# Graph attention on one core: key weights and x alternate in the load queue, a second bank and stage for the last two folded quads, and a reordered opening and tail

## The reference

```python
h = relu(layernorm(x))                     # no scale, no shift, eps 1e-5
q, k, v = h @ W_q.T + b_q, h @ W_k.T + b_k, h @ W_v.T + b_v
z = (q @ k.T) / sqrt(512) * adj
z = where(z == 0, -10000, z)
out = x + relu(softmax(z, axis=1) @ v)
```

## Time and profile before

| | us |
|---|---|
| runs, median of 3 | 1481.22 (1480.55 to 1481.66) |
| the profiled execution's own time | 1482.13 |
| its span in the profile | 1480.3 |
| PE busy | 1461.4 (99%) |
| DVE busy | 1301.0 (88%) |
| ACT busy | 868.7 (59%) |
| POOL busy | 44.7 (3%) |
| moved by DMA | 301.24 MB, mean 203 GB/s |

### The profile page before, as it was taken

One profiled execution on the slowest core, in us unless ns is written; L12 is line 12 of the kernel. 1 busy time (PEld: TensorE's weight loads), 2 busy tenths in 40 slices (PEclk: granted clock), 3 DMA queues, 4 the chain that ended last, 5 costly groups with the idle time before them and its releaser, 6 DMA issues.

```text
span 1480.3 us, 24626 instructions
## 1 busy us (share of the span) xinstructions
PE 1461.4 (99%) x9414; PEld 927.0 (63%) x9414; DVE 1301.0 (88%) x1595; ACT 868.7 (59%) x1398; POOL 44.7 (3%) x27
## 2 busy tenths in 40 slices
PE   8999999999999999999999999999999999999998
PEld 4556665666666666666666666666666666666443
DVE  6877887898999999898989899989999899988985
ACT  3666665765666556655656565655665566555541
POOL 0000000000001000100010000000010001000100
PEclk9999999999999999999999999999999999999999
DMA  5445534465555665566655565656566555664252
GB/s 206 153 171 211 187 141 178 172 233 212 228 200 217 227 242 213 195 244 221 228 210 219 221 237 213 233 220 221 213 242 227 219 199 213 227 221 181 91 169 87
DMA packets 75045, 301.24 MB, mean 203 GB/s; under 512 B 8496, under 2 KB 8496, under 8 KB 73136
## 3 DMA queue, kind: packets, MB, share of 16 engines
q1 hardware_dynamic: 74928, 299.66, 54.3%
HBM read 260.84 MB, written 38.80 MB: 202 GB/s over the span
## 4 chain that ended last, share of the span: by engine, by line
PE 94%; DVE 3%; ACT 1%; issue 1%; DMA 0%; SPq 0%; POOL 0%; DVEq 0%; ACTq 0%
PE o L604 44%; PE za L552 22%; PE zd L552 11%; PE zb L552 5%; PE o L525 5%; PE o L539 4%; PE o L507 1%; PE za L613 0%; PE o L623 0%; DVE g_buf L1090 0%; DMA slots<-in_L_gnn_W_k 0%; DVE slots L1206 0%; ACT g_buf L740 0%; PE zb L613 0%; DVE slots L1177 0%
## 5 line engine op out<-in xcount | busy, mean ns | idle before, releaser
L604 PE MATMUL o<-v_buf,p_buf 128*128 128x512 f16 x3072 | 734.2, 379 | 0.8 <-DVE p_buf L1213 0.6
L604 PEld LDWEIGHTS o<-v_buf,p_buf 128*128 128x128 f16 x3072 | 300.5, 98 | 270.8 <-issue 1.5
L552 PE MATMUL za<-h_buf,g_buf 128*128 128x256 f16 x2952 | 402.2, 273 | 5.2 <-DVE g_buf L1090 2.2
L552 PEld LDWEIGHTS za<-h_buf,g_buf 128*128 128x128 f16 x2952 | 287.5, 98 | 143.3 <-ACT mm_tmp L767 3.6
L552 PE MATMUL zd<-h_buf,g_buf 128*128 128x256 f16 x1476 | 201.3, 273 | 0.0
L806 ACT ACTIVATE slots<-slots,log_p 128x1024 f32<-128x1024 f32 x128 | 146.0, 1141 | 56.6 <-DVE slots L1206 56.6
L1206 DVE TENSOR_TENSOR slots<-slots,floor_b 128x1024 f32<-128x1024 f32 x128 | 170.0, 1330 | 0.3 <-POOL floor_b L480 0.3
L1213 DVE TENSOR_TENSOR p_buf<-slots,p_buf 128x1024 f16<-128x1024 f32 x128 | 157.4, 1230 | 13.7 <-PE o L604 13.4
L1169 DVE TENSOR_TENSOR slots<-um_tmp,dm_tmp 128x512 f32<-128x512 f32 x128 | 89.2, 697 | 82.3 <-ACT dm_tmp L794 82.3
L801 ACT ACTIVATE slots<-za,c_all,kappa 128x256 f32<-128x256 f32 x128 | 72.3, 565 | 143.1 <-PE za L552 142.1
L1181 DVE SCALAR_TENSOR_TENSOR slots<-slots 128x1024 f32<-128x1024 f32 x128 | 156.0, 1219 | 0.2
(11 more groups left out here) (141 smaller groups left out, 1127.4 us busy)
## 6 DMA issues: line engine op xcount, KB each, us to landing
g_buf<-g_dram SPq DMA_DIRECT2D x108, 896.0 KB, 5.2
v_buf<-v_dram SPq DMA_DIRECT2D x128, 512.0 KB, 3.3
adj_own<-in_adj SPq DMA_DIRECT2D x92, 512.0 KB, 6.1
spare<-in_adj SPq DMA_DIRECT2D x36, 512.0 KB, 6.2
g_dram<-g_buf SPq DMA_DIRECT2D x12, 896.0 KB, 4.4
v_dram<-v_buf SPq DMA_DIRECT2D x16, 512.0 KB, 5.4
spare<-in_x SPq DMA_DIRECT2D x15, 512.0 KB, 8.1
h_buf<-h_dram SPq DMA_DIRECT2D x7, 1024.0 KB, 9.1
```

The lines of the kernel that those rows point to most:

```text
L552: mm = pe.matmul(bank[:, 0:QH], g_of(i)[:, a, op, j, :], right[b][j], start=(fresh and j == 0 and m == 0), stop=(j == 1 and m == 2), skip_ ...
L604: mm = pe.matmul(o_bank[t][:, :], a[:, kt, span], v_buf[:, n % V_BUFS, kt, b, :], start=(j == 0 and kt == 0 and m == 0), stop=(j == PAIRS ...
```

## The change

It reorders the opening's loads and first products, gives the projections of quads 6 and 7 a second bank and a second stage, spreads the statistics of quads 2 and 3 over two steps each, moves the first minima of block 1 and exp(2) and exp(3) behind other work, and halves the last output tile by columns. The lines of the diff that matter, with the surrounding lines cut; the renamed semaphores and the replacement of `g_stage` by `stage_of(q, j)` in `high_g`, `combine_g` and `low_g` are left out:

```diff
@@ -133,6 +133,8 @@
 h_keep = in_slots(2, 2).rearrange("p (k n) -> p k n", k=KC)
+g_stages = [g_stage, p_buf[:, 0:4, :, :].rearrange("p a t n -> p (a t n)").bitcast(F32)
+            .rearrange("p (o u n) -> p o u n", o=8, u=2)]
@@ -310,6 +313,10 @@
     return min(n + 2 + (j >= 6) + (j >= 10), STEPS - 1)
+def seen_by(n):
+    return PAIRS + n if n < 4 else PAIRS + 5 if n == 4 else n + LEAD - 1
@@ -319,6 +326,16 @@
     return pair if i % 2 == 1 and 0 <= pair < PAIRS else -1
+def late_quad(q):
+    return q >= QUADS - 2
+def gT_bank(q, i):
+    return o_bank[1] if late_quad(q) and i % 2 == 1 else o_bank[3]
+def stage_of(q, j):
+    return g_stages[j if late_quad(q) else 0]
@@ -394,13 +411,14 @@
         sp.dma_start(out_quads[s][:, a:a + 2, :], o_rows[:, a:a + 2, :]).then_inc(stored[a // 2], 16)
-    for j, b in enumerate((bq, bk)):
-        sp.dma_start(b_cols[:, j, :], b.rearrange("(k p) -> p k", p=P),
-                     allow_slow_non_contiguous=True).then_inc(bias_loaded, 16)
-    for t in range(QUAD):
-        sp.dma_start(x_quad[0][:, t, :], x_quads[0][:, t, :]).then_inc(x_first_loaded[t], 16)
+    sp.dma_start(b_cols[:, 0, :], bq.rearrange("(k p) -> p k", p=P),
+                 allow_slow_non_contiguous=True).then_inc(bq_loaded, 16)
...
+        sp.dma_start(x_quad[0][:, e, :], x_quads[0][:, e, :]).then_inc(x_first_loaded[e], 16)
+        if e == 1:
+            sp.dma_start(b_cols[:, 1, :], bk.rearrange("(k p) -> p k", p=P),
+                         allow_slow_non_contiguous=True).then_inc(bk_loaded, 16)
@@ -455,13 +473,17 @@
     last = BLOCKS - 1
-    for t in range(QT):
+    for t in range(QT - 1):
...
+    for c in range(2):
+        cols = slice(c * DIM // 2, (c + 1) * DIM // 2)
+        sp.wait_ge(finished, QUAD * last + QT + c)
+        sp.dma_start(out_quads[last][:, QT - 1, cols], o_rows[:, QT - 1, cols]).then_inc(stored[QT - 1], 16)
...
-    sp.wait_ge(stored[3], 16)
+    sp.wait_ge(stored[3], 32)
@@ -531,12 +553,15 @@
             pe.wait_ge(v_lo_ready, 4)
+        elif late_quad(q) and i > 0:
+            pe.wait_ge(h_lo_ready, TILES)
+            pe.wait_ge(g_copied, KC * q + i - 1)
...
-                mm = pe.matmul(gT_bank[:, :], m_pair[:, a, k, c * P:(c + 1) * P], h[:, b, k, :],
+                mm = pe.matmul(gT_bank(q, i)[:, :], m_pair[:, a, k, c * P:(c + 1) * P], h[:, b, k, :],
@@ -599,11 +624,19 @@
         span = slice(t * P, (t + 1) * P)
-        for kt in range(2):
-            for m, (a, b) in enumerate(((p_hi[n % 3], 0), (p_hi[n % 3], 1), (p_lo[n % 2], 0))):
-                mm = pe.matmul(o_bank[t][:, :], a[:, kt, span], v_buf[:, n % V_BUFS, kt, b, :],
-                               start=(j == 0 and kt == 0 and m == 0),
-                               stop=(j == PAIRS - 1 and kt == 1 and m == 2))
+        pieces = ((o_bank[t][:, :], 0, DIM),)
+        if s == BLOCKS - 1 and t == QT - 1:
+            pieces = ((o_bank[t][:, 0:DIM // 2], 0, DIM // 2), (b_bank[:, 0:DIM // 2], DIM // 2, DIM))
+        if n == STEPS - PAIRS and t == QT - 1:
+            pe.wait_ge(m2_copied, STEPS)
+        for bank, c, d in pieces:
+            for kt in range(2):
+                for m, (a, b) in enumerate(((p_hi[n % 3], 0), (p_hi[n % 3], 1), (p_lo[n % 2], 0))):
+                    mm = pe.matmul(bank, a[:, kt, span], v_buf[:, n % V_BUFS, kt, b, c:d],
+                                   start=(j == 0 and kt == 0 and m == 0),
+                                   stop=(j == PAIRS - 1 and kt == 1 and m == 2))
+            if n == STEPS - 1 and d < DIM:
+                mm.then_inc(o_half_done, 1)
@@ -622,16 +655,17 @@
     mm.then_inc(w_ready, 1)
+    product_m(0)
...
-    product_m(0)
-    transpose_h(2)
-    transpose_h(3)
+    pe.wait_ge(bk_loaded, 16)
...
+    transpose_h(2)
+    transpose_h(3)
@@ -724,10 +758,14 @@
         act.wait_ge(gT_ready, KC * q + i + 1)
-        act.wait_ge(g_lo_ready, 4 * q + 2 * (i // 2))
-        to = g_stage[:, A11:A21 + 1:A21 - A11, :, :] if i % 2 == 0 else g_stage[:, A12:A22 + 1, :, :]
+        if late_quad(q) and q == QUADS - 1:
+            act.wait_ge(g_lo_ready, 4 * q + 2 * (i // 2) - 2)
+        elif not late_quad(q) or i // 2 == 0:
+            act.wait_ge(g_lo_ready, 4 * q + 2 * (i // 2))
+        stage = stage_of(q, i // 2)
+        to = stage[:, A11:A21 + 1:A21 - A11, :, :] if i % 2 == 0 else stage[:, A12:A22 + 1, :, :]
...
-                             gT_bank[:, :].rearrange("p (u t n) -> p u t n", u=2, t=2),
+                             gT_bank(q, i)[:, :].rearrange("p (u t n) -> p u t n", u=2, t=2),
@@ -836,10 +874,10 @@
     square_root(0)
+    act.wait_ge(w_ready, 1)
+    nc.scalar.copy(w_all, w_bank[:, :]).then_inc(w_copied, 1)
...
-    act.wait_ge(w_ready, 1)
-    nc.scalar.copy(w_all, w_bank[:, :]).then_inc(w_copied, 1)
@@ -892,16 +930,14 @@
             high_t(0, 2 * (k - 5) + 1)
-        if k == 7:
-            square_root(3)
...
-        if k in (1, 2):
-            high_m(2 * k - 2)
-            high_m(2 * k - 1)
+        if k in (2, 3):
+            high_m(2 * k - 4)
+            high_m(2 * k - 3)
...
-        if i == 2 and g + 2 < QUADS and g != 1:
+        if i == 2 and g + 2 < QUADS:
@@ -934,8 +970,6 @@
     copy_d(LEAD)
-    exp(2)
-    high_p(2)
@@ -951,7 +985,9 @@
             copy_o(s, 0)
-        if soon and not first:
+        if n == 1:
+            exp(2)
+        elif soon and not first:
@@ -959,7 +995,9 @@
             copy_m7(n + LEAD)
-        if soon and not first:
+        if n == 1:
+            high_p(2)
+        elif soon and not first:
@@ -972,7 +1010,7 @@
             copy_d(n + LEAD)
-        if first:
+        if first or n == 1:
@@ -1282,19 +1320,20 @@
     dve.wait_ge(zeros_ready, 1)
-    dve.wait_ge(bias_loaded, 32)
+    dve.wait_ge(bq_loaded, 16)
...
-    v.tensor_tensor(bias_product[:, :], b_cols[:, 0, :], b_cols[:, 1, :], ALU.mult).then_inc(bias_product_ready, 1)
-    dve.wait_ge(bias_product_ready, 1)
-    v.tensor_reduce(bias_part[:, :], bias_product[:, :], AX_X, ALU.add).then_inc(bias_part_ready, 1)
...
+    dve.wait_ge(bk_loaded, 16)
+    v.tensor_tensor(bias_product[:, :], b_cols[:, 0, :], b_cols[:, 1, :], ALU.mult).then_inc(bias_product_ready, 1)
+    dve.wait_ge(bias_product_ready, 1)
+    v.tensor_reduce(bias_part[:, :], bias_product[:, :], AX_X, ALU.add).then_inc(bias_part_ready, 1)
@@ -1320,11 +1359,6 @@
     quad_rstd(1)
-    for t in range(2 * QUAD, 3 * QUAD):
-        row_stats(t)
-    for t in range(2 * QUAD, 3 * QUAD):
-        aggregate(t)
-    quad_var(2)
@@ -1338,7 +1372,7 @@
             add_c2(whole)
-        if i == 3 and g + 2 < QUADS and g != 1:
+        if i == 3 and g + 2 < QUADS:
@@ -1366,17 +1400,15 @@
             link(v.tensor_scalar(u_cols[:, :], u_cols[:, :], up[1][:, 0:1], None, ALU.mult))
-        if k == 7:
-            quad_rstd(3)
...
-        if k in (1, 2):
-            low_m(2 * k - 2)
-            low_m(2 * k - 1)
+        if k in (2, 3):
+            low_m(2 * k - 4)
+            low_m(2 * k - 3)
@@ -1390,9 +1422,13 @@
             combine_t(1, k - 29)
-        if (i == 1 and g >= 2 or k == 6) and g + 2 < QUADS:
+        if g < 2 and i < 2:
+            row_stats(QUAD * (g + 2) + 2 * i)
+            row_stats(QUAD * (g + 2) + 2 * i + 1)
+        if g >= 2 and i == 1 and g + 2 < QUADS:
...
+        if i == 1 and g + 2 < QUADS:
@@ -1431,13 +1467,11 @@
     low_p(1)
-    see_min(PAIRS + 1)
...
-    see_min(LEAD - 1)
@@ -1471,7 +1505,8 @@
         if scored:
-            see_min(i - 1)
+            for m in range(seen_by(n - 1) + 1, seen_by(n) + 1):
+                see_min(m)
@@ -1489,13 +1524,25 @@
     last = BLOCKS - 1
-    for t in range(QT):
+    for t in range(QT - 1):
...
+    t = QT - 1
+    for c in (0, DIM // 2):
+        if c == 0:
+            dve.wait_ge(o_half_done, 1)
+        else:
+            dve.wait_ge(o_done, QT * STEPS)
+        part, cols = o_rows[:, t, c:c + DIM // 2], slice(c, c + DIM // 2)
+        v.scalar_tensor_tensor(out=part, in0=o_bank[t][:, cols] if c == 0 else b_bank[:, 0:DIM // 2], scalar=row_out[:, t:t + 1],
+                               in1=bv_all[:, cols], op0=ALU.mult, op1=ALU.add).then_inc(biased, 1)
+        dve.wait_ge(biased, QUAD * last + t + 1 + (c > 0))
+        v.scalar_tensor_tensor(out=part, in0=part, scalar=0.0, in1=x_tail[:, 1, cols],
+                               op0=ALU.max, op1=ALU.add).then_inc(finished, 1)
...
```

More of the change, by code:

```diff
@@ L168, in adj_preln_attention @@
         wq_loaded = [sem(f"wq_loaded{e}") for e in range(KC)]
-        bias_loaded = sem("bias_loaded")
+        bq_loaded = sem("bq_loaded")
+        bk_loaded = sem("bk_loaded")
         bv_loaded = sem("bv_loaded")
@@ L739, in high_g @@
                         act.wait_ge(g_stored[pair % G_OPEN], 16 * (pair // G_OPEN))
-                    nc.scalar.copy(g_of(pair)[:, 0, :, j, :], g_stage[:, 0:OPS, u, :]).then_inc(g_hi_ready, 1)
+                    nc.scalar.copy(g_of(pair)[:, 0, :, j, :], stage_of(q, j)[:, 0:OPS, u, :]).then_inc(g_hi_ready, 1)
             def high_t(s, k):
```

(5 more changed lines are left out.)

9 lines of the change are left out of this document (2 added, 7 removed).

## The result

The changed kernel takes 1478.45 us (median of 14 executions, 1476.51 to 1479.93). The kernel before takes 1481.59 beside it (median of 14, 1480.55 to 1482.33). The ratio is 0.9979, with an interval of 0.9971 to 0.9988: 3.1 us faster, where 7.2 were forecast. It lies above the range, which ended at 1477.4. The profiled execution took 1478.43 us with a span of 1476.4 us, against 1482.13 and 1480.3 before.

The account below looks back on a forecast made before the run. TensorE's work was taken as the bound, so only its standstills or half clock could yield: -3.3 - 1.4 - 2.6 + 0.15 = -7.2 us from 1482.13 gives 1474.9, or 1474.0 from the runs' median; 8-in-10 range 1471.8 to 1477.4.

Parts of the forecast that it names:

- part 2: Statistics of quads 2 and 3 by twos in the loop: a new stall takes 3.2 us, later two waits go.
- rival A: At the start, TensorE's clock falls as it works in bursts between landings: 1476.1 us; chance 0.20.
- part 3: Second bank and stage for quads 6 and 7, at 248 to 273 us: 1.4 us won, ends 0 and 2.1.
- The waits at 70.68 and 77.61: TensorE's waits for a value tile (1.03 us) and the first folded operand (1.15 us), to go with quad 3's statistics by twos.
- parts 1 and 2: Opening up to the first score, which was to begin at 74.3 instead of 77.61: 3.3 us won, ends 1.0 and 4.5.
- What is late next: After the quad 7 stalls: low_g(7,1) for pair 14, TensorE coming to it at 279.8 and it being done at 279.7.
- Part 4: Block 1's first minima moved behind other work: two TensorE stalls in step 1 go, 2.6 us won, ends 1.3 and 2.8.
- Part 5: Last output tile halved, in the last block and tail: 0.15 us lost, ends -0.4 and +0.8.
- rival D: Slower: 96 more weight loads in block 7's quarter with 256 columns, 9.4 us if shown in full, 1483.4; chance 0.03.
- Rival B: VectorE takes back some 2.5 of the 4.0 us of parts 3 and 4: 1476.5 us; chance 0.12.
- Rival C: Stall before project_g(0,0) longer, or queue order moves no landing; opening gains 0: 1477.3 to 1478.5 us; chance 0.07.
- part 1: Queue order and order of first products at the start: TensorE reaches the first value tile 4.4 us ahead, at 30.7.

Follow-up runs that it names:

- e1_warm: The changed kernel with 13 small products on zeros where TensorE stands still in step 4 of the loop over k; 1476.54 us.
- e2_stats_ahead: The changed kernel with quad 2's statistics back ahead of the loop over k and the splits of M back in steps 1 and 2; 1474.74 us.

## Why the prediction was wrong

**The step that failed** is the one in part 2: "3.2 of the 4.4 us go back in a new stall at about 46 to 49 us and 1.1 stay". The stall was there, in the place and nearly with the length that was worked out: 1.36 + 1.67 = 3.03 us instead of 3.2. What the prediction did not ask is what this standstill does to the clock. It had asked exactly that of the start (rival A), and left it out 40 us later, at a stall that it had itself made. So the price of the stall went into the sum as its length alone. The granted clock falls to 0.50 there and `project_g(0, 0)` costs 1.69 us more; e1_warm gives 1.67 of it back at the first score and 1.9 in the median, and its 1476.54 lies inside the range. Three of the changed kernel's fourteen executions (1476.51 to 1477.06 us, mean clock 1.000) do so too. The rest of the shortfall is smaller and spread: 0.9 us in the opening and 0.5 in part 3.

Point by point:

- **The start (rival A, 0.20)** went as the forecast had it. Key products from 4.98 us (about 4.8 was said), clock 1.00 throughout, transposes at 14.85 (14.2 to 14.6), first value tile at 31.11 (30.7), a lead of 3.80 us over the 34.91 of the timeline before, where 4.4 over 35.1 were said. The bursts between landings, with pauses of 1.28, 0.24 and 0.23 us, did not bring the clock down.
- **`project_g(0, 0)`** came at 49.66, not 49.0. VectorE's chain was 0.5 us late already at `low_v(0)` (34.52 instead of 34.0), which waits for the first value tile, itself 0.4 us late, and kept that until the last low half ended, at 49.56. The product began 0.1 us after that. The sum had a slip as well: 34.0 and 15.2 to 15.3 us of work give 49.2 to 49.3, not 49.0. Measured from 34.52 the work was 15.0 us.
- **The waits at 70.68 and 77.61** are gone, as forecast; this half of part 2 measured 2.07 us. With the clock's 1.67 us, parts 1 and 2 brought 0.69 us where 3.3 were summed: 0.66 of the gap from the later start, 1.69 from the clock, and about 0.3 from the steps between, which e1_warm still has (its first score comes at 75.25, 0.95 after the 74.3 of the forecast, 0.66 of it from the later start).
- **Part 3: a term mis-sized.** The stalls at 261.78 and 272.57 were worth 1.40 us, from a lead of 0.69 to one of 2.09, which is the forecast to the digit, and the one at 250 was worth nothing. "What is late next" was sought in the low half at the start of pair 14. It was the copy that frees the bank for that pair's last piece: `copy_m1` of pair 15, queued ahead of it, waits for VectorE's `add_c11`, and 0.43 to 0.5 us go back. Net 0.9 by the spans, 0.5 by the medians.
- **Part 4** was 2.63 us by the ledger and 2.3 by the medians, 2.6 forecast.
- **Part 5** cost 0.26 to 0.5 us, 0.15 forecast: the two halves ended 0.31 us later than a whole tile, not 0.2. The loads of block 7 are hidden (0.66 us for six products of 256 columns), so rival D is out.
- **Rival B** took back a part of part 3 and nothing of part 4. **Rival C** named the right place and the wrong mechanism: the stall was not longer, but what followed it ran at half clock. That the measured 1478.45 lies in rival C's span of 1477.3 to 1478.5 is luck.
- **The base.** The sum was made against 1482.13 and then lowered by 0.9. By medians the whole forecast was 7.2 and the outcome 3.1; e2_stats_ahead, which has all parts but the harmful half of part 2, brought 6.35. The lower end of the range, 1471.8, is not what its words give: part 1 at 4.5 and parts 3 to 5 half way to their ends make 1472.1. It decided nothing.
